# First attention of a two-layer block: exponentials split into f16 halves and turned by DMAs, division moved behind the product with the values, and the work placed anew over the steps

## The reference, cut to what matters

```python
q = (_layernorm(x) @ wq.T + bq)        # x: 2 x 2048 x 512, 16 heads of 32
k, v = ctx @ wk.T + bk, ctx @ wv.T + bv  # ctx: 2 x 154 x 512
scores = clip(q k^T / sqrt(32), -100, 100)     # where mask == 0: -inf
attn = softmax(scores, axis=-1)
x = x + tanh(g_xattn[0]) * ((attn @ v) @ wo.T + bo)
```

## Time and profile before

| | |
|---|---|
| median of 3 runs | 2790.43 us (2787.85 to 2791.42) |
| profiled execution, its own time | 2809.87 us |
| its span in the trace | 2808.1 us |
| busy share of the span: PE, DVE, ACT, POOL | 94%, 57%, 51%, 37% |
| mean granted TensorE clock | 0.984 of 2.4 GHz |

### The profile page before, as it was taken

One profiled execution on the slowest core, in us unless ns is written; L12 is line 12 of the kernel. 1 busy time (PEld: TensorE's weight loads), 2 busy tenths in 40 slices (PEclk: granted clock), 3 DMA queues, 4 the chain that ended last, 5 costly groups with the idle time before them and its releaser, 6 DMA issues. The chain is left out here.

```text
span 2808.1 us, 44981 instructions
## 1 busy us (share of the span) xinstructions
PE 2644.7 (94%) x16990; PEld 1473.8 (52%) x16990; DVE 1594.4 (57%) x2629; ACT 1425.9 (51%) x3586; POOL 1042.0 (37%) x823
## 2 busy tenths in 40 slices
PE   5999988999999989999999979999999999999999
PEld 3554544444444457777777645565444444444444
DVE  6888885655555346655656568988543422333222
ACT  3888885323222146666666548999443222322221
POOL 1455451465555636666766500111102201221111
PEclk8999999999999999999999989999999999999999
DMA  6221214222222269999999842321420110011000
GB/s 186 52 85 57 74 31 169 61 61 61 75 70 54 76 215 289 285 296 282 288 288 289 207 101 76 91 44 42 157 64 16 46 42 34 16 46 46 19 12 30
DMA packets 287479, 311.17 MB, mean 111 GB/s; under 512 B 155169, under 2 KB 164129, under 8 KB 287265
## 3 DMA queue, kind: packets, MB, share of 16 engines
q1 hardware_dynamic: 250400, 240.96, 27.0%
q0 software_dynamic: 36864, 67.34, 11.7%
HBM read 198.86 MB, written 75.89 MB: 98 GB/s over the span
## 5 line engine op out<-in xcount | busy, mean ns | idle before, releaser
L1376 POOL DMA_INDIRECT ids<-sh_tk,sh_su x256 | 269.8, 1054 | 243.9 <-PE sh_gu L55 70.5
L55 PE MATMUL ex_gu<-ex_xT,ex_h 128*128 128x256 f16 x3072 | 347.5, 273 | 4.6 <-issue 3.8
L55 PEld LDWEIGHTS ex_gu<-ex_xT,ex_h 128*128 128x128 f16 x3072 | 301.2, 98 | 53.9 <-issue 4.4
L1775 POOL DMA_INDIRECT xp<-ex_oo,ex_to x128 | 242.3, 1893 | 178.6 <-ACT ex_oo L1683 123.2
L2323 POOL TENSOR_TENSOR fe_prodT<-fe_pp,fe_prodT 128x512 f16<-128x512 f32 x64 | 77.5, 1210 | 591.2 <-ACT fe_prodT L2108 591.2
L521 PE MATMUL at_g<-id,at_p 128*128 128x128 f32 x1280 | 205.1, 288 | 38.7 <-POOL at_p L901 30.7
L1510 DVE SCALAR_TENSOR_TENSOR ex_h<-ring,ex_h 128x1024 f16<-128x1024 f32 x128 | 151.1, 1222 | 153.0 <-ACT ex_h L1500 153.0
L521 PEld LDWEIGHTS at_g<-id,at_p 128*128 128x128 f32 x1280 | 164.9, 169 | 106.9 <-issue 41.7
L680 ACT ACTIVATE at_s<-at_s,at_mx 128x154 f32<-128x154 f32 x512 | 210.4, 417 | 0.0
L900 POOL TENSOR_TENSOR at_p<-at_s,at_rs 128x1024 f32<-128x1024 f32 x64 | 121.5, 1898 | 223.3 <-DVE at_rs L800 223.3
L55 PE MATMUL at_g<-hm_zT,hm_w 128*128 128x512 f16 x768 | 182.1, 389 | 19.8 <-issue 12.5
(11 more groups left out here) (331 smaller groups left out, 5407.8 us busy)
## 6 DMA issues: line engine op xcount, KB each, us to landing
ring<-L_ffn_expert_gate_up_w SPq DMA_DIRECT2D x64, 1024.0 KB
ring<-L_ffn_expert_down_w SPq DMA_DIRECT2D x64, 512.0 KB
ring<-x SPq DMA_DIRECT2D x24, 1024.0 KB, 5.8
x<-ring SPq DMA_DIRECT2D x16, 1024.0 KB, 4.7
zrows<-hm_zs SPq DMA_DIRECT2D x32, 256.0 KB
xp<-ring SPq DMA_DIRECT2D x8, 1024.0 KB
out<-ring SPq DMA_DIRECT2D x8, 1024.0 KB, 4.3
ring<-xp SPq DMA_DIRECT2D x7, 1024.0 KB, 5.7
```

The lines of the kernel that those rows point to most:

```text
L55: mm = nc.tensor.matmul(out, lhs(a, k), rhs(b, k), start=start and i == 0 and j == 0, stop=stop and i == n - 1 and j == 2)
L1376: e.indirect_dma_start(ids, bass.IndirectOffsetOnAxis(slotu[b % 2][:, t, j:j + 1], 0), pair[b % 2][:, t, j, :], None, bounds_check=SLOTS - ...
L1775: e.indirect_dma_start(dst, bass.IndirectOffsetOnAxis(to[:, n:n + 1], 0), o32[y % 2][:, t, :], None, bounds_check=T + SLOTS - 1, oob_is_er ...
```

## The change

The function `attention`, which served both attentions, becomes `first_attention` and `second_attention`. The second keeps its instructions. In the first:

- The exponentials have no accumulator and are not multiplied by anything. A copy makes the high f16 half in `prob` (two buffers, `high`: ACT for even units, DVE for odd ones), POOL subtracts it to make the low half, and SP turns each half by one DMA transpose of 128x1280 f16 (`turn_keys`). The 10 transposes on PE and the three copies go.
- V, VR and the turned exponentials are pairs of f16 halves. A `values` piece has 3 times 4 products of 32 columns and 3 whole ones, and then 2 times 4 and 2 products with ones, which give the sums. ACT takes their inverse by Ln and Exp, DVE multiplies (`divide`, one step later), ACT copies the f16 half, and POOL subtracts for the low half (`halve`, two steps later).
- `low` goes from DVE to POOL for all blocks but the first.
- The table of the steps is new. `oT` has two buffers, and `finish` of a block may lie two steps further on.

```diff
-        TURNS = ((-10, -10, -9, -9), (-7, -6, -5, -4) if L0 else (-8, -7, -4, -3))
-        VALS, FIN = ((7, 8, 11, 12), (13, 13, 14, 14)) if L0 else ((6, 7, 10, 11), (12, 12, 13, 13))
+        VALS, FIN = (7, 8, 11, 12), (15, 16, 17, 18)
+        Z, LOW = (-14, -14, -10, -10), (-13, -13, -9, -9)
...
+                proj = (-5, -4, -3, -2)
...
+                at(n + m + 1, "divide", b, what)
+                at(n + m + 2, "halve", b, what)
...
-                    e.wait_ge(s["p_act"], by_scalar * unit)
-                    e.wait_ge(s["p_vec"], (3 - by_scalar) * unit)
-                    for j in range(HG):
-                        o = grp * P + j * HD
-                        e.matmul(out[j * HD:(j + 1) * HD, :], V[g][:, o:o + HD], ptb[:, place(gi * HG + j), :],
-                                 start=True, stop=False)
-                    e.matmul(out[:, :], VR[g][:, grp, :], ptb[:, HH + gi, :], start=False, stop=True).then_inc(s["o_mm"], 1)
+                    for i in range(unit - NP, unit):
+                        e.wait_ge(*keys_landed(i))
+                    for hv, hp in TERMS:
+                        for rows, k in heads:
+                            e.matmul(out[rows, :], V[g][:, hv, o:o + HD], ptb[:, hp, k, :],
+                                     start=(hv, hp) == TERMS[0], stop=False)
+                    for hv, hp in TERMS:
+                        mm = e.matmul(out[:, :], VR[g][:, hv, grp, :], ptb[:, hp, HH + gi, :], start=False,
+                                      stop=(hv, hp) == TERMS[-1])
+                    for hp in range(2):
+                        for rows, k in heads:
+                            e.matmul(out[rows, :], each[:, :], ptb[:, hp, k, :], start=hp == 0, stop=False)
+                    for hp in range(2):
+                        mm = e.matmul(out[:, :], every[:, :], ptb[:, hp, HH + gi, :], start=False, stop=hp == 1)
...
+                    e.activation(recip[n % 2], bank_of["d", n][:, :], ACT.Ln).then_inc(s["d_ln"], 1)
+                    e.activation(recip[n % 2], recip[n % 2], ACT.Exp, scale=-1.0).then_inc(s["d_inv"], 1)
...
+            def high(i):
+                if not 0 <= i < UNITS or i % 2:
+                    return
+                e.wait_ge(s["expd"], 2 * i + 2)
+                if i >= NP:
+                    e.wait_ge(*keys_landed(i - NP))
+                e.copy(first_keys(prob[0][:, 0, :]), sc[i % NS][:, :, 0:P])
+                e.copy(last_keys(prob[0][:, 0, :]), rest_of(i)).then_inc(s["p_hi0"], 1)
...
+                    e.wait_ge(s[f"p_hi{i % 2}"], i // 2 + 1)
+                    e.tensor_tensor(first_keys(rows[:, 1, :]), sc[i % NS][:, :, 0:P], first_keys(rows[:, 0, :]), ALU.subtract)
+                    e.tensor_tensor(last_keys(rows[:, 1, :]), rest_of(i), last_keys(rows[:, 0, :]), ALU.subtract
+                                    ).then_inc(s["p_lo"], 1)
...
+            def turn_keys(i):
+                for h, made in enumerate(((s[f"p_hi{i % 2}"], i // 2 + 1), (s["p_lo"], i + 1))):
+                    e.wait_ge(*made)
+                    e.dma_start_transpose(pT[i // TPB % 2][:, h, :, t * P:(t + 1) * P], prob[i % NP][:, h, :]
+                                          ).then_inc(s[f"keys{i % NP}"], 16)
```

More of the change, by code:

```diff
@@ L444, in attention @@
[L444 to L448, removed]
-            early = 2 if b == 1 else 3 if L0 or b == 2 else 4
-            if b:
-                for i in range(2 if L0 else 3):
-                    at(max(n + turns[0] - early - (2 if L0 or b < 3 else 4) + i, 0), "stats", b, i)
-            for t in range(TPB):
-                for lead, what in ((-early, "prepare"), (1 - early, "low"), (-1, "turn")):
-                    if b:
-                        at(n + turns[t] + lead, what, b, t)
-                if L0 and b < NB:
-                    at(n + t, "bias", b, t)
+                for i in range(2):
+                    at(-1, "stats", 0, i)
@@ new lines, in first_attention @@
+                for t in range(0, TPB, 2):
+                    for what in ("prepare", "low"):
+                        at(-1, what, 0, t)
+                        at(-1, what, 0, t + 1)
+                at(-1, "split", 0, 0)
+                at(-1, "keys", 0, 0)
+                for t in range(TPB):
+                    at(-1, "turn", 0, t)
+                at(-1, "biases", 0, 0)
+                at(-1, "split", 1, 0)
+                at(3, "keys", 1, 0)
+                for i, m in enumerate((0, 1, 4, 5)):
+                    at(m, "value_rows", i // 2, i % 2)
@@ L466, in attention @@
             for t in range(TPB):
                 at(n + FIN[t], "finish", b, t)
-        for i, m in enumerate((1, 2) if maps_ahead else ()):
-            at(UNITS + m, "maps", 0, i)
-        for i, m in enumerate((5, 5, 5) if rows_ahead else ()):
-            plan[UNITS + m].append(("split_ahead", 0, i))
-        rank = dict(split_ahead=0, low=0, turn=2, prepare=3)
+        for i in range(3):
+            plan[UNITS + 5].append(("split_ahead", 0, i))
+        rank = dict(split_ahead=0, low=0, prepare=0, values=1, finish=2, turn=5)
@@ L628, in piece @@
             def piece(what, B, k):
-                nm, b, n = whose(B, 0 if what == "values" else k)
+                nm, b, n = whose(B, k if what in ("stats", "prepare", "low", "finish") else 0)
                 if what == "stats":
@@ new lines, in keys @@
+            def keys(g):
+                for m in range(KT):
+                    e.wait_ge(s["k_mm"], KT * g + m + 1)
+                    src_ = bank_of["k", g, m]
+                    if g == 0 and m == 0:
+                        e.wait_ge(s["kbias_in"], 16)
+                    o = e.tensor_scalar(KTn[g][:, m, :], src_[:, 0:CTX], bk[:, m:m + 1], None, ALU.add)
+                    o.then_inc(s["k_out"], 1)
+            for g in range(BATCH):
+                e.memset(VR[g][:, :, :, :], 0.0)
```

827 lines of the change are left out of this document (539 added, 288 removed).

## The result

The changed kernel takes 2844.1 us (median of 4 runs, 2838.11 to 2847.68) against 2790.57 us: a ratio of 1.0191, 95% interval 1.0173 to 1.021. It is slower by 1.9%, where 0.6% faster was predicted; 2844 also lies outside of the range (2750 to 2802). Its profiled execution took 2843.61 us, with a span of 2841.8. The attention ends at 522.52 us where it ended at 471.64. The code behind it is the same, but lasted 2309 to 2353 us in the profiles of this study, which ran on several chips; the attention of the kernel before ended at 469.04 us in a second profile.

The account below looks back on a forecast made before the run. PE was nearest to a bound, no engine full. Larger loads, corrected to 44.4, plus clock 1.6 and POOL's loop 0.5 gave 46.5 us a block; -3, six times -3.0, -4, +7 made -18: 2773 us, range 2750 to 2802.

Parts of the forecast that it names:

- Middle block: One repeating block of eight steps in the first attention: 46.5 us forecast, range 44.4 to 50, before 49.5.
- sums by the larger load: Middle block: adding each step's larger load of PE and DVE gave 50.2 us before (49.5 measured), 44.9 after.
- The ring: PE takes its four PSUM tiles `at_g` strictly in turn; the prediction had no wait from this.
- the counterpart of L770: DVE's `divide`, in place of the values' product that waited 43.4 us in all for ACT; it comes a step later.
- the 1.6 us for the clock: Middle block: PE's clock falls in most blocks after waits in steps 1 and 2, costing 1.6 us a block.
- the dear 32-column products: Rival in `values` pieces: five groups cost twice a whole pass; 49.0 us a block, 2789 us in all; chance 5%.
- DMA has room: Middle block: the mean DMA share is 0.24 before the change, so transfers have room.
- nobody waits for them: Turned keys land within 3.6 us of their issue, hidden with 1 to 3 us to spare, so no engine waits.
- Units 0 to 7: Start of the first attention, 58.8 us before, DVE the bound: 3 us less (0 to 6).
- Last units: Units 56 to 62, 39.35 us before: 35.5 with 2 for a cold clock, so 4 less (0 to 6).
- Tail: From the last clip to the barrier, 35.2 us before: 42.5, so 7 more (3 to 10).
- POOL as the bound: Rival in middle blocks: POOL's subtraction and DVE's copies slow each other; about +20 us, 2810; chance 15%.

Follow-up runs that it names:

- the best version: Changed kernel with DVE's divide before the clip, next part's weights later, POOL's halves before its subtraction, block 1's turns in step 3: 0.9949 of the kernel before.
- That 0.58: The best version with one turn of keys a unit, low halves of the turned rows left out: 0.9925 of the kernel before, 46.5 us a block.

## Why the prediction was wrong

- **Middle block, 46.5 predicted, 55.8 measured.** The step that failed is the check at its head: "sums by the larger load" were right to 2% before, and I used them for a program in which buffers are held over other spans. The sum counts how long engines work, and lets PE and DVE couple only by scores and clip. The ring couples them again (`d` on `o`, 5.5 to 6.6 us a block), and POOL's order a third time (`halve` behind a subtraction that waits for DVE, 2.9 to 4.0 us). I wrote that the counterpart of L770 "comes a step later now" and took it for a gain; I did not ask what stays occupied for that step. With both waits mended and nothing else in the middle blocks changed, they take 46.2 us. That this is so near to 46.5 is partly luck: the 1.6 us for the clock in the 46.5 were worth 0.3 at most there, and a cost of z stands in no term (both below).
- **Its terms, partly right by offsetting errors.** POOL's unit is 2.06 and 0.60 (2.35 and 0.66 predicted), busy for 35.3 us of a block for 39.7. DVE's whole load in a block of the best version came out at 41.2 (41.9 predicted). The exponentials took 0.33 apart (0.3), the `values` piece 2.5 from its start to the next piece (2.3), so the dear 32-column products are refuted; the turn 1.35 to issue and 3.6 to land (1.6 and 3.6).
- **DVE beside POOL.** DVE's `high` is 0.95 in place of 1.4. I had taken POOL as busy nearly always while DVE copies. But POOL's next subtraction waits for this very copy, so in the changed kernel POOL stood idle in 29 of the 32 copies of 1024 columns, which took 684 ns. The one that lay wholly beside POOL's work in the best version took 1834 ns. With z it is the other way round: it fell more often beside POOL's work, and rose from 540 ns to 890, and to 1437 in units 8 to 55 of the best version. These are 3.6 us of DVE a block that I had left out, since I took the earlier trace rows without asking what POOL does meanwhile. By instruction, z takes about 540 ns with POOL idle (31 of 32 before, 18 of 32 in the changed kernel). Wholly beside POOL's work it took 1427 ns on average in the changed kernel (12 of 32) and 1437 in the best version (20 of 32). The Trainium skill's page "GPSIMD Engine Reference" (section 8, Key points) says that the two share SBUF interfaces; I had applied that to the mask and the copy, and not to z. Timeline of the best version, a pair of z, and the copy beside POOL's work:

```profile
174.70 1.46 POOL L826 TENSOR_TENSOR at_oT<-at_wv,at_oT 128x512 f16<-128x512 f32 x1
175.18 3.45 DVE L148 TENSOR_SCALAR hm_z<-ring,at_mv,at_rstd 128x512 f32<-128x512 f32 x2
176.12 2.23 POOL L842 TENSOR_TENSOR at_p<-at_s,at_p 128x1024 f16<-128x1024 f32 x1
...
405.50 2.06 POOL L842 TENSOR_TENSOR at_p<-at_s,at_p 128x1024 f16<-128x1024 f32 x1
...
406.28 1.83 DVE L758 CAST at_p<-at_s 128x1024 f16<-128x1024 f32 x1 [0.44 <-ACT at_s L646]
...
407.51 1.02 POOL L843 TENSOR_TENSOR at_p<-at_s,at_p 128x208 f16<-128x208 f32 x1
```

- **The clock.** I gave it +1.6 us a block. It falls, after waits of PE: mostly three times a block in the changed kernel (mean 0.89 in units 16 to 55) and once or twice in the best version (0.95). With idle matmuls that hold it at 0.99 the mean block is 0.3 us shorter, and the five blocks shown take the same time (229.00 and 229.25 us). The term is 0 to 0.3 in the best version, with the open end on the keys said above. What the clock costs on top of the two waits in the changed kernel was not measured by itself.
- **DMA has room.** The forecast was right in effect, for a poor reason. I took the mean share of 0.24 as room without adding the new turns: it is 0.93 in the best version. That 0.58 is no faster shows that room in time was left even so. But my "nobody waits for them" is wrong: a copy of the high half waited for keys once on DVE (3.4 us) and once on ACT (1.9) in blocks 1 to 6 of the changed kernel, and five times on ACT (9.0 us in all) in the best version.
- **Units 0 to 7, -3 predicted, +5.6 measured.** DVE's gain was sized right: with SP's order mended it is -3.7. I had looked at SP's queue in a middle block only; in block 1 turns of rows stand behind keys, mask and load.
- **Last units, -4 predicted, -3.3 measured.**
- **Tail, +7 predicted, +12.7 measured.** The mechanism was seen (three weights ahead of the last copy), its size was not: the last `values` ended 22.3 us after the clip (19.8), and the weights then waited 2.2 us for their load, so the last copy came 30.9 us after the clip for 25.8, and PE waited 12.1 in place of 8. With the weights behind the copy the tail was 7.4 us shorter (48.8 to 41.4), which is still longer than 35.2.
- **POOL as the bound** was the rival that ended slower. It named the right sign by a mechanism that is absent: POOL's subtraction took 2.66 us a unit on average where that rival needed 4.2, and POOL had waited 185 us ahead of it.

Of the 51 us, the two waits in six blocks are 58 (9.6 each), the start 9, the weights 7; against them stand about 23 us of gain. In the version with all mended the attention ends at 448.06, 23.6 us earlier than in the profile of before, and the kernel is faster by 0.5% (0.9949, 15.9 us). That is near the 0.6% predicted for the change, but it is the result of another program. Of the 8 us between 23.6 and 15.9, 2.6 are the spread of the two profiles of before; the rest stays open.

## What to carry to other kernels

When a result is consumed later than before, list what it holds meanwhile (a tile of a ring, a slot of a buffer) and walk the ring in the new order for one period: with n tiles taken in turn, the nth piece after it waits for that consumer, wherever it stands. A sum of loads by step is reached only when each engine's in-order list has its inputs in that order; on each engine a piece whose input is old goes ahead of one whose input is fresh. Read queue order in the first and the last block by themselves, since the middle one tells nothing of them. And before a row's price is carried over, ask for each piece whether the other engine works or waits while it runs: the copy that POOL waits for ran at the price that it has alone, the z beside which POOL works did not.

## What the hardware showed besides

- The same DVE instruction (z, 128x512 f32, one operand in SBUF) took 533 to 548 ns when POOL was idle in the changed kernel, and 565 to 2283 wholly beside POOL's work in the best version. In units 16 to 55 its mean was 540, 1018 and 1399 ns in the kernel before, the changed one and the best. What counts is where it falls, not POOL's share: before, POOL was busy for 51% and never beside it in these units. In the same profile `divide` (0.68) and the maxima (0.79) took the same beside POOL as without it.
- A turn of 128x1280 f16 took 2.0 us of all 16 DMA engines: the share of 0.93 less 0.58 over 262 us is 92 us, for the 45 turns left out there (8 in each of 5.7 blocks). Yet at a share of 0.93 the block was no longer than at 0.58, although single copies and products waited for keys. The Trainium skill's page "Perfetto Trace Analysis" (Identifying the Most-Contended Engine) calls occupancy misleading for DMA, since there are 16 engines; the trace agrees.
- Code that is the same, behind the attention, took 2309 to 2312 us in four profiles on one chip and 2340 to 2353 in eight on three others. The changed kernel's attention, on that fast chip and on the first one (2319 behind it), had the same 55.8 us a block: the chips' difference sits in the part behind the attention.
